# Attention score jobs of a two-layer transformer kernel: visits of two or three pairs, in any free pair of banks

## The reference

```python
x = L0_attn_x
xn = _layernorm(x, axis=-1)
x = x + _L0_attn_ref(xn, ...) + _L0_ffn_ref(xn, ...)
xn = _layernorm(x, axis=-1)
x = x + _L1_attn_ref(xn, ...) + _L1_ffn_ref(xn, ...)
# attention, both layers: 32 heads of 16 channels, causal
scores = jnp.einsum('bhqd,bhkd->bhqk', q, k)
weights = jax.nn.softmax(jnp.where(causal, -jnp.inf, scores) / 4, axis=-1)
ctx = jnp.einsum('bhqk,bhkd->bhqd', weights, v)      # then @ Wo + bo
# feed-forward: 1792 wide in layer 0 (after an RMS norm), 1376 in layer 1
y = (silu(xn @ gate_w.T) * (xn @ up_w.T)) @ down_w.T
```

## Time and profile before

| | before |
|---|---|
| median of 3 runs | 852.76 us |
| profiled execution | 853.96 us |
| its span, first to last instruction | 851.8 us |
| mean granted TensorE clock | 0.990 |
| TensorE busy | 823.5 us, 97% |
| VectorE busy | 556.8 us, 65% |
| ScalarE busy | 460.6 us, 54% |
| GpSimd busy | 414.4 us, 49% |

### The profile page before, as it was taken

The page is one execution under the profiler, slowest core; times in us unless marked ns, Lnnn a source line. Parts: engine busy times, 40 slices in busy tenths (PEclk is TensorE's granted clock), DMA queues, the critical chain, the costliest instruction groups (busy, mean ns, idle before and its releaser), DMA issues.

```text
span 851.8 us, 16321 instructions
## 1 busy us (share of the span) xinstructions
PE 823.5 (97%) x5596; PEld 625.1 (73%) x5596; DVE 556.8 (65%) x1576; ACT 460.6 (54%) x824; POOL 414.4 (49%) x551
## 2 busy tenths in 40 slices
PE   8999999998999999999999999998998899999997
PEld 4877666787876766777678766775676777676787
DVE  7866555588675578656577786456566676655355
ACT  3453555575655556546566575444565465545653
POOL 4543554446544444454445444557554445444451
PEclk9999999998999999999999999999999999999999
DMA  6757345453527263644766275565747385833241
GB/s 214 197 172 165 102 112 147 85 134 89 138 88 153 86 139 113 126 148 92 182 117 174 94 125 187 111 186 94 214 98 188 103 153 189 147 118 89 89 114 62
DMA packets 66321, 113.60 MB, mean 133 GB/s; under 512 B 13240, under 2 KB 16312, under 8 KB 66232
## 3 DMA queue, kind: packets, MB, share of 16 engines
q1 hardware_dynamic: 66240, 112.57, 52.5%
HBM read 87.57 MB, written 24.90 MB: 132 GB/s over the span
## 4 chain that ended last, share of the span: by engine, by line
PE 82%; DVE 9%; DMA 4%; issue 2%; SPq 1%; ACT 1%; POOL 0%; DVEq 0%; ACTq 0%
PE g_ring L1269 39%; PE acc L1269 23%; PE g_ring L1422 8%; PE s_bank L1382 7%; PE t_bank L1402 4%; DVE s_bank L1236 2%; DMA o_scratch<-o_t 1%; DMA w_raw<-weights_in 1%; DVE x L1223 1%; DMA m_scratch<-m_rows 1%; DVE h L1145 1%; DVE xt_lo L1156 1%; DVE xt_lo L1159 1%; SPq L871 1%; DVE h_lo L1210 1%
## 5 line engine op out<-in xcount | busy, mean ns | idle before, releaser
L978 POOL TENSOR_TENSOR w_lo<-w_raw,w_hi 128x512 fp32r<-128x512 f32 x204 | 268.5, 1318 | 162.0 <-ACT w_hi L1022 158.2
L1236 DVE CUSTOM_DVE_ANT_0 s_bank<-s_bank,causal 128x128 f32<-128x128 f32 (+3 forms) x512 | 236.9, 518 | 39.1 <-PE s_bank L1382 38.9
L1002 POOL TENSOR_SCALAR_AFFINE_SELECT p<-p 128x256 f32<-128x256 f32 (+1 forms) x320 | 122.9, 386 | 259.3 <-ACT p L1015 252.4
L1269 PE MATMUL g_ring<-xt_hi,w_hi 128*128 128x512 f32 (+1 forms) x504 | 208.9, 414 | 2.0 <-DVE qk_parts L1168 1.1
L1269 PE MATMUL g_ring<-xt_lo,w_hi 128*128 128x512 f32 (+1 forms) x504 | 197.5, 392 | 0.0
L1269 PE MATMUL g_ring<-xt_hi,w_lo 128*128 128x512 f32 (+1 forms) x504 | 197.0, 391 | 0.0
L1022 ACT ACTIVATE w_hi<-w_raw 128x512 fp32r<-128x512 f32 x204 | 127.5, 628 | 118.4 <-PE g_ring L1269 82.0
L1015 ACT ACTIVATE p<-t_bank 128x512 f32<-128x512 f32 x320 | 173.8, 595 | 21.2 <-PE t_bank L1402 14.0
L1269 PE MATMUL acc<-w_hi,h_hi 128*128 128x256 f32 (+1 forms) x528 | 157.4, 298 | 5.9 <-DVE h_lo L1210 5.3
L1269 PE MATMUL acc<-w_lo,h_hi 128*128 128x256 f32 (+1 forms) x528 | 150.7, 285 | 0.0
L1269 PE MATMUL acc<-w_hi,h_lo 128*128 128x256 f32 (+1 forms) x528 | 150.5, 285 | 0.0
(11 more groups left out here) (86 smaller groups left out, 789.2 us busy)
## 6 DMA issues: line engine op xcount, KB each, us to landing
w_raw<-weights_in SPq DMA_DIRECT2D x204, 256.0 KB, 3.1
qk_scratch<-qk_parts SPq DMA_DIRECT2D x24, 512.0 KB, 3.9
q_op<-qk_scratch SPq DMA_DIRECT2D x96, 128.0 KB, 4.6
o_scratch<-o_t SPq DMA_DIRECT2D x32, 256.0 KB, 2.8
k_op<-qk_scratch SPq DMA_DIRECT2D x48, 128.0 KB, 7.4
context<-o_scratch SPq DMA_DIRECT2D x16, 256.0 KB
inverse<-r_scratch SPq DMA_DIRECT2D x16, 256.0 KB
k_op<-k_scratch SPq DMA_DIRECT2D x48, 64.0 KB, 5.0
```

What stands on the lines that cost most here:

```text
L978: pool.tensor_tensor(w_lo[:, c % SPLIT, :], w_raw[:, c % RAW, :], w_hi[:, c % SPLIT, :].bitcast(F32), ALU.subtract).then_inc(split_done, 1)
L1002: pool.affine_select(out=view, in_=view, compare_op=ALU.is_ge, fill=0.0, base=0, pattern=[[0, n], [1, P]] if n == 2 else [[1, P]], channel ...
L1236: last = dve.tensor_tensor_reduce(out=bank[:, at:at + n], in0=bank[:, at:at + n], in1=causal[:, 512 - n:], scale=1.0, scalar=LOWEST, op0=A ...
L1269: ins = pe.matmul(dst, w[a], xa[c], start=first and i == 0, stop=last and i == 2, skip_group_check=skip)
```

## The change

- A visit is a list of two or three pairs. The pairs stand in one sequence PAIRS, S and T in turn, in the order in which the visits had them. visit_of(m) takes up to WIDE = 3 from it: each gets the pair of banks that comes free earliest by the planner's clock. The second is left out if it would be over ALONE = 4.0 us late, the third if it is not ready at once.
- Three pairs of banks ("slots") are free to any S, T or Mt: s_bank (0), t_bank (1), and, while no output group is open, acc (2). acc_user notes who had an acc bank, so that its next user waits for that one's reduction or exponential.
- Mt takes the slot that is free first, and mrow reads it there.
- A unit's PV is put behind the first visit step after its last T pair, not behind a fixed one.
- The planner's cost of a visit is 0.36 + 0.25 for each pair (0.75 before), the due time of a T pair is half a visit later, and a late step is taken ahead of dense work only if it is ready within 0.5 us (1.5 before).

The matmuls, reductions, exponentials and transfers are the same in number and shape. The order's text has 131 visit steps, 73 of two pairs and 58 of three, 74 of them with a pair in acc.

```diff
-PV_LATER = 0
+PAIRS = pair_order()
+WIDE = 3
...
-    def visit_ready(v):
...
+    def slots_by_time():
+
+        times = [(after("slot", 0), 0), (after("slot", 1), 1)]
+        if not state["open"]:
+            a = state["acc"]
+            times.append((max(freed("acc", a, 2), freed("acc", a + 1, 2)), 2))
+        return sorted(times)
+
+    def visit_of(m):
...
+        for n, item in enumerate(PAIRS[m:m + min(WIDE, len(times))]):
+            r = max(pair_ready(*item), times[n][0])
+            if n == 0 and r == NEVER and held_pv(m) is not None:
+                break
+            if n == 2 and r > max(state["t"], ready) + NEAR:
+                break
+            if n == 1 and r > max(state["t"], ready) + ALONE:
+                break
+            ready = max(ready, r)
+            taken.append(item + (times[n][1],))
+        return taken, ready
...
     def mtrans(u):
-        e = end["Mt", u] = pe_step(end["smax", u], "Mt", u)
+        free, slot = slots_by_time()[0]
...
+        e = end["Mt", u] = pe_step(max(end["smax", u], free), "Mt", u, slot, a, before)
...
-        elif late and min(late)[1] < max(can, t + 1.5):
+        elif late and min(late)[1] < max(can, t + 0.5):
...
+            def wait_slot(slot, a, before):
+
+                if slot == 2:
+                    wait_acc(a)
+                    wait_acc(a + 1)
+                elif before == "early":
+                    pe.wait_ge(g_freed, max(last_early[2 * slot], last_early[2 * slot + 1]))
+                else:
+                    wait_pair(*before)
...
                 elif kind == "ST":
-                    v = s[1]
...
+                    for what, p, slot, a, before in s[1]:
+                        wait_slot(slot, a, before)
+                        banks = pair_banks(slot, a)
+                        u, jobs = jobs_of(p)
```

## The result

The changed kernel takes 831.42 us (median of four runs, 830.16 to 834.11) against 852.71 us: a ratio of 0.972, 95% interval 0.9686 to 0.9754 (the two medians alone give 0.975). The forecast was 841.5 us, a ratio of 0.987. So the direction was right and the time lies inside the range, but the gain was far too small: 21 us against 11 us by the medians, and by the ratios 2.8% against 1.3%, over twice. The profiled execution took 834.11 us, 832.0 us of it span, so the two spans differ by 19.8 us. (The runs of before that stood beside the later experiments had medians of 854 to 856 us; each experiment is given with the ratio to its own.)

The account below looks back on a forecast made before the run. The prediction took TensorE's work and its few waits to bound the kernel. From the profiled 853.96 us, terms of -8.5, -5.4 and +1.5 us gave 841.6 us; it predicted 841.5 us, range 829 to 852.

Parts of the forecast that it names:

- What bounds the kernel: Whole kernel: the time is TensorE's work plus its little standing still; TensorE busy 823.5 of 851.8 us, VectorE 556.8 us.
- First term: Visits on TensorE: 36 fewer visits, with a third pair at 0.36 us, take 149.9 us down to 141.4 us: -8.5 us.
- The drain on a change of tiling mode: Entry and exit of visits: changing tiling mode drains TensorE, none between pairs; 0.20 us left over after the pairs agrees.
- Second and third term: TensorE's waits: -5.4 us for waits and low clock that go, +1.5 us for added waits on gate's product and accumulator pair.
- waits on rows of maxima: Scores behind the maxima's transpose: different banks end their wait for VectorE's read, -2.8 + 0.6 = -2.2 us.
- The wait at the accumulator pair: Output tiles after a visit: a lent accumulator pair must be drained before the next group; 1.0 us charged at one place.
- I leave it as it is: Remaining waits (VectorE behind with output tiles, h_lo, two DMA returns): visits stay at two pairs there, so no change counted.
- The gate's product: Projections after a visit of three: VectorE's doubled score reductions delay the product that frees a projection bank, 0.5 us added.
- The other edits issue nothing; they only choose the order: Planner's visit estimates, due times and 0.5 in place of 1.5: they issue nothing, only choose the order already counted.
- All goes well: Rival, about 832 us: third pair at 0.30 us, all bank waits and their low-clock stretches gone; chance 0.16 (below 836).
- Nothing reaches the end: Rival, about 853 us: draining banks bound the kernel, so the 8.5 us turn into waits; chance 0.12.
- Slower by stalls: Rival: visits of three stall TensorE's in-order queue until their third bank is free; 7 such waits give 862.6 us; chance 0.07.

Follow-up runs that it names:

- The doubled scores: The kernel before with every S pair computed twice in a row into the same banks, 160 pairs more: 886.7 us (one run).

## Why the prediction was wrong

- *What bounds the kernel*: right. TensorE's work and waits are the whole of the change; VectorE's and ScalarE's lists are no shorter, and no new engine limits.
- *First term, -8.5 us*: the mechanism was right (fewer entries and exits, 36 visits fewer), the size was off; -11.9 us measured, -11.3 us from the visits' costs. Two steps failed, in opposite directions. The third pair was put at 0.36 us, "the pair in the midst of a visit", but in a visit of two none stands in the midst; each borders on an entry or an exit. The doubled scores measured 0.254 us, which over 58 visits is 6.1 us more of gain. And all visits were charged an entry and an exit of their own, though 58 of 167 before and 45 of 131 after stand beside a PV and save one border; at some 0.19 us each that is 2.5 us less of gain. The bound from one pair to two, 0.30 us, would have given -12.0 us. It is the nearer row, but that its sum comes out so well is luck: it is too dear by as much as the borders at the PV take back.
- *The drain on a change of tiling mode*, told beside the first term, fits further than was thought there. The Trainium skill, page TensorEngine Tiling (Array Packing), Key Properties, ties the drain to a change of mode. This agrees with the rows at the PV too. A PV works on column tiles and the pairs on row tiles, and the last pair in front of a PV takes 0.32 us, as in front of full-array matmuls.
- *Second and third term, -5.4 us and +1.5 us, waits and clock*: too small by half; -4.4 us of waits and -3.5 us of clock in the profiled executions. Right were two places: waits on rows of maxima went from 2.8 to 0.3 us (0.6 us forecast), the one behind back-to-back visits vanished. But the transpose's own wait for the last maxima, put at nothing, grew from 0.6 to 3.5 us, more than the forecast's -2.2 us: the wait moved from behind the transpose to before it. And the reason given, the transpose's free bank, is not borne out: with its bank fixed again the waits on rows of maxima stayed at 0.3 us. The wait at the accumulator pair came as forecast, 1.29 us where 1.0 us was charged, and a second one of 0.6 us (TensorE's timeline of after):

```profile
385.84 0.40 PE L1498 MATMUL s_bank<-q_op,k_op 50*128 50x256 f32 x4
387.53 0.39 PE L1351 MATMUL acc<-w_hi,h_hi 128*128 128x256 f32 x1 [1.29 <-DVE maxima L1318]
```

- What failed there is "I leave it as it is". The waits for an output tile's operand fell by 3.1 us, the longest of them, 3.1 us in rows 6, is gone, and so is the low clock behind it. Of the 4.9 us for a reduced bank, of which the forecast took out 1.5 us, 4.4 us went. The forecast priced waits one by one and took the scattered ones to stay. With free banks and up to three pairs, all waits together are 3.9 to 7.5 us below those of before in five of six orders; with free banks and two pairs they are not. What it is in the wider visits that spares them stays open.
- *The gate's product, 0.5 us of the third term*: right. One projection waits 1.0 us for it, where one waited 0.3 us.
- *"The other edits issue nothing; they only choose the order"*: true, and the largest gap in the working. With 1.5 us for late steps the changed kernel's order is over 11 us slower, and the kernel before gains nothing from 0.5 us; with the old banks the new planner costs 14 us.
- *Rivals.* "All goes well (832 us)" gave the time, with half of its grounds: the third pair was even cheaper than its 0.30 us, but by no means all waits went. That it meets 831.42 us is in part luck. "Nothing reaches the end", by draining banks, is refuted for the changed kernel: visits of three do not wait for a bank at their third pair more than 0.5 us in all. Slower by stalls were only kernels of two pairs a visit without a third pair of banks. A sign that was to show the forecast wrong, a new stretch of granted clock below 0.9, did appear, 0.57 in 344 to 348 us behind a wait of 1.7 us for the return of the maxima, without the time suffering in all.

Open is what sets the clock's part. The low stretches follow waits: after the transpose's wait at 189.00, the clock is 0.86 and 0.71 of full speed (stretches of after):

```profile
188.00:192.00 4.00, 2.56 (x13) 1.93 (x14) 3.48 (x14) 1.76 (x4) 1.93 (x3) 0.86 0.15 30
192.00:196.00 4.00, 4.00 (x26) 4.00 (x26) 2.93 (x4) 2.28 (x7) 3.00 (x3) 0.71 0.13 46
```

But not each wait is followed by one: the clock stays full after the 1.24 us at 434.26 before (rows 7) and the 1.29 us at 387.53 after. And executions of one kernel, with one order of instructions, differ by up to 8.6 us in the clock's part. No run here separates what decides whether a wait of 1 to 2 us is followed by a low stretch. Nor was it tried which of the waits would vanish if the order were held word for word and only the banks changed: every change of banks deals a new order.

## What to carry to other kernels

Price a step that is to be packed tighter by its marginal cost, in the middle of three, and not from one that borders on the switch into or out of its mode; where no run of three exists, the difference of one and two is the nearer row. Count the borders between one kind of tile and the next, not the steps: a visit beside a PV has one border fewer to lose, and removing it saves less (0.22 us by the fit, against 0.37 us for one that stands alone). And where a planner deals the order of five engines, an edit of its numbers is not free: leave a term of some 10 us to either side for waits and the low clock behind them, or nudge a number that means nothing and see what the order alone does.

## What the runs showed of the hardware

- Two 512-wide matmuls on the two halves of the array, in a row of such pairs, take 0.24 us, four on 128 and 384 or on 256 columns 0.24 to 0.29 us; the first pair after full-array matmuls takes 0.33 to 0.39 us until the next starts. Going from the full array to such pairs and back costs some 0.37 us in all. Going from such a pair to a PV, on four column tiles, costs about as much as going to the full array: the pair before it takes 0.32 us.
- The time lost to the granted clock, between 2.4 and 1.2 GHz, differs between executions of one kernel: 3.4 to 12.0 us in 41 executions of the kernel before, 0 to 5.0 us in four of the changed one. The means of the kernels, with TensorE's waits between 16 and 31 us, go from 1.7 to 14.3 us. One profiled execution is therefore no measure of it.
